# A fused LayerNorm, gated recurrence and Fourier mixing layer: the recurrence moves from a stage between two passes into the passes' tile slots

## What is computed

```python
xn    = (x - mean) / sqrt(var + eps) * ln_gamma + ln_beta        # per token
delta = sigmoid(xn @ w_delta + b_delta)                          # 16 states per token
B_t   = xn @ w_in + b_in
gate  = sigmoid(xn @ w_gate + b_gate)                            # 512 x 512
h     = tanh((h * delta[t]) @ A + B_t[t])                        # over the 2048 tokens of a sequence
x1    = layernorm(x + (h @ C) * gate + x)
w     = complex(w_freq_real, w_freq_imag)                        # 512 x 512, sparse
y     = real(ifft(fft(x1) @ w)) + bias                           # = x1 @ M + bias, with one real M
out   = layernorm(x1 + y)
```

## Time and profile before

| | |
|---|---|
| median of 3 runs (lowest, highest) | 897.38 us (897.34, 898.28) |
| profiled execution: span, which is the time it shows of itself | 897.9 us |
| PE, DVE, ACT, POOL busy | 869.1, 722.7, 566.1, 554.1 us (97%, 80%, 63%, 62%) |
| first gate product of pass A, last one's end | 23.86, 404.24 us |
| first product with M of pass B | 477.27 us |
| HBM read, written | 140.53, 67.11 MB |

### The profile page before, as it was taken

One profiled execution on the slowest core, in us unless ns is written; L12 is line 12 of the kernel. 1 busy time (PEld: TensorE's weight loads), 2 busy tenths in 40 slices (PEclk: granted clock), 3 DMA queues, 4 the chain that ended last, 5 costly groups with the idle time before them and its releaser, 6 DMA issues.

```text
span 897.9 us, 17982 instructions
## 1 busy us (share of the span) xinstructions
PE 869.1 (97%) x5275; PEld 470.4 (52%) x5306; DVE 722.7 (80%) x1510; ACT 566.1 (63%) x1063; POOL 554.1 (62%) x890
## 2 busy tenths in 40 slices
PE   7899999999999999999988999999999999999996
PEld 5354545454545444448764555555555555555553
DVE  5978888888888899885678888888888888888883
ACT  3334444444444456664645888888888888888887
POOL 2656666666665665541236677777777777777782
PEclk9999999999999999999999999999999999999999
DMA  8487788888887777526034666676677667666743
GB/s 301 141 282 281 269 295 308 323 288 287 294 297 273 272 263 263 193 95 235 1 84 147 234 227 234 241 271 217 235 259 252 218 238 272 238 233 232 259 164 141
DMA packets 94530, 210.04 MB, mean 234 GB/s; under 512 B 3616, under 2 KB 5920, under 8 KB 90528
## 3 DMA queue, kind: packets, MB, share of 16 engines
q1 hardware_dynamic: 94208, 209.41, 66.7%
q10 hardware_dynamic: 288, 0.21, 0.1%
HBM read 140.53 MB, written 67.11 MB: 231 GB/s over the span
## 4 chain that ended last, share of the span: by engine, by line
PE 54%; issue 18%; POOL 15%; DVE 7%; ACT 3%; DMA 2%; POOLq 1%; another core or an unknown queue 0%; DVEq 0%; ACTq 0%
PE bank L1344 13%; PE bank L1345 13%; PE bank L1347 13%; POOL lo_sb L711 8%; PE bank L1334 6%; PE bank L1510 3%; POOL a_rstd L698 2%; DMA x_sb<-x 2%; PE bank L1401 2%; POOL diag L706 2%; DVE bn L1002 1%; PE bank L1461 1%; PE bank L1454 1%; DVE xs_sb L1034 1%; DVE h_lo L1190 1%
## 5 line engine op out<-in xcount | busy, mean ns | idle before, releaser
L711 POOL TENSOR_TENSOR lo_sb<-xs_sb,hi_sb 128x512 f16<-128x512 f32 x128 | 150.5, 1176 | 140.0 <-ACT hi_sb L494 140.0
L754 POOL TENSOR_TENSOR x_sb<-x_sb,gate_sb 128x512 f32<-128x512 f32 x128 | 164.0, 1282 | 76.8 <-DMA x_sb<-x 60.6
L494 ACT ACTIVATE hi_sb<-xs_sb 128x512 f16<-128x512 f32 x128 | 80.6, 629 | 202.0 <-DVE xs_sb L1034 195.2
L1344 PE MATMUL bank<-wg_hi,hi_sb 128*128 128x512 f16 x512 | 194.4, 380 | 8.2 <-POOL wg_lo L716 5.6
L1345 PE MATMUL bank<-wg_lo,hi_sb 128*128 128x512 f16 x512 | 194.7, 380 | 0.0
L1344 PE MATMUL bank<-z_sb,hi_sb 128*128 128x512 f16 x512 | 194.3, 379 | 0.4 <-DVE w_ring L1241 0.4
L1345 PE MATMUL bank<-z_sb,hi_sb 128*128 128x512 f16 x512 | 194.2, 379 | 0.0
L1039 DVE SCALAR_TENSOR_TENSOR lo_sb<-bank,hi_sb 128x512 f16<-128x512 f32 x128 | 88.5, 692 | 75.5 <-ACT hi_sb L637 75.3
L1347 PE MATMUL bank<-wg_hi,lo_sb 128*128 128x512 f16 x512 | 131.4, 379 | 0.0
L1347 PE MATMUL bank<-z_sb,lo_sb 128*128 128x512 f16 x512 | 131.4, 379 | 0.0
L637 ACT ACTIVATE hi_sb<-bank 128x512 f16<-128x512 f32 x128 | 76.3, 596 | 67.8 <-PE bank L1334 67.5
(11 more groups left out here) (189 smaller groups left out, 1361.2 us busy)
## 6 DMA issues: line engine op xcount, KB each, us to landing
x_sb<-x SPq DMA_DIRECT2D x63, 1024.0 KB, 6.1
gate_dram<-gate_sb SPq DMA_DIRECT2D x32, 1024.0 KB, 5.3
gate_sb<-gate_dram SPq DMA_DIRECT2D x32, 1024.0 KB, 6.2
out<-out_sb SPq DMA_DIRECT2D x31, 1024.0 KB, 5.3
h_sb<-x_turned SPq DMA_DIRECT2D x16, 1024.0 KB, 7.3
norm_sb<-x_turned SPq DMA_DIRECT2D x15, 1024.0 KB, 7.3
h_rep<-fourier_constants SPq DMA_DIRECT2D x2, 514.0 KB, 6.1
x_sb<-x SPq DMA_DIRECT2D x2, 512.0 KB, 6.1
```

Of the source, the lines that this page charges most:

```text
L711: pool.tensor_tensor(lo_sb[:, k % 4], xs_sb[:, k % 2], hi_sb[:, k % 4], ALU.subtract).then_inc(s_lo, 1)
L754: pool.tensor_tensor(x_sb[:, k // 4, k % 4], x_sb[:, k // 4, k % 4], gate_sb[:, k // 4, k % 4], ALU.add).then_inc(s_v, 1)
L1344: nc.tensor.matmul(dst, hi_sb[:, slot_of, t], w_hi[:, t], start=(t == 0), stop=False)
```

## The change

The sequences' tokens are cut in two halves (groups) of 1024; group 0 holds partitions 0 to 63 of the state tiles and group 1 the other 64. A group's recurrence has 64 lanes by 2 column blocks, so a step still has 128 columns, and there are 32 steps for each group: 64 in all, against 32 before. The step's matrix now has a shift beside A, so that one matmul takes z and the state together (L1454 goes). One step stands in each slot: group 0 in slots 70 to 101 of pass A, group 1 in slots 5 to 36 of pass B. In a slot the matmul is the first thing on PE, tanh the first on ACT, and the product with delta the last on DVE. The check of the ends, the branch and the split into fp16 halves follow in slots 102 to 108 and 37 to 43.

M's weights are folded first (POOL, slots 52 to 66), which leaves 8 pairs of products, each of twelve matmuls of about 256 columns, in slots 85 to 111 (`PAIR_SLOTS`); ACT, DVE and POOL combine them in the slots behind. The preparations on DVE that stood in slots 104 to 124 stand in slots 48 to 80 (`PREPARATION`). Pass B's slots -7 to 2 run inside pass A's slots 121 to 130. The copies into `h_rep` are 16 DMAs for each group, in SP's order behind the gates of octet 13 and behind pass B's octet 5. The loops cover fewer octets (4 of 16 in pass A, 7 of 16 in pass B). The general rounds stay behind a branch, now one for each group.

```diff
-LANES = SEQ // CHUNK
-STEPS = 2 * CHUNK
+GROUP = SEQ // 2
+LANES = GROUP // CHUNK
...
+A_WRITTEN, B_WRITTEN, B_LAST = 5, 7, OCTETS - 2
+
+SCAN_FIRST = (70, 5)
+SCAN_CHECK = tuple(n + 2 * CHUNK for n in SCAN_FIRST)
+SCAN_BRANCH = tuple(n + 2 for n in SCAN_CHECK)
+SCAN_SPLIT = tuple(n + 1 for n in SCAN_BRANCH)
+
+PAIR_SLOTS = (85, 87, 93, 95, 101, 103, 109, 111)
...
+        m = n - TILES
+        if m >= first_b:
+            slot_b(m, m % 8, m // 8)
...
+                if v == OCTETS - 3:
+                    sp.wait_ge(s_split[0], 1)
+                    replicate_states(0)
+                    sp.dma_start(h_before[ROWS:P], h_sb[0:ROWS, :, GROUP - CHUNK:GROUP]).then_inc(s_hbefore, 16)
...
+            def scan_tanh(g, count, s):
+                act.wait_ge(s_pre[g], count)
+                nc.scalar.activation(h_sb[scan_rows(g), :, s::CHUNK],
+                                     ps_scan[g][scan_rows(g), 0:2 * LANES].rearrange("p (q l) -> p q l", q=2),
+                                     ACT.Tanh).then_inc(s_h[g], 1)
...
+            def scan_product(g, s):
+
+                rows = scan_rows(g)
+                nc.vector.tensor_tensor(zh_sb[rows, g, :, s + 1::CHUNK], h_sb[rows, :, s::CHUNK],
+                                        del_sb[rows, :, s + 1::CHUNK], ALU.mult).then_inc(s_hd[g], 1)
...
+            def scan_step(g, count, s):
+                pe.wait_ge(s_hd[g], count)
+                nc.tensor.matmul(ps_scan[g][:, 0:2 * LANES].rearrange("p (q l) -> p q l", q=2), scan_a[:],
+                                 zh_sb[:, g, :, s::CHUNK], start=True, stop=True).then_inc(s_pre[g], 1)
...
-            def slot(n, k, v):
+            def slot_b(n, k, v):
+                scan_slot(1, n)
                 if exists(n + 1):
                     transpose(n + 1, k + 1, s_bnorm, s_bhi, s_blo, s_bt)
-                if isinstance(n, int) and n + 7 < 8:
-                    first_states_out(n + 7, (k + 7) % 8)
-                elif exists(n + 7):
+                if exists(n + 7):
                     states_out(n + 7, (k + 7) % 8, v if k < 1 else v + 1)
```

More of the change, by code:

```diff
@@ L428, in second_pass @@
             def second_pass(v, q):
-                sp.wait_ge(s_v, v * 8 + 4 * q + 4)
+                if isinstance(v, int) and v == 0:
+                    sp.wait_ge(s_gst[q], 16 * OCTETS)
+                else:
+                    sp.wait_ge(s_v, v * 8 + 4 * q + 4)
                 load_gate(v + 1, q)
-                if not isinstance(v, int):
+                if before(v, 1):
                     store_result(v - 1, q)
@@ new lines, in scan_until_settled @@
+            def scan_until_settled(g):
+                act.wait_ge(s_flag[g], 1)
+                changed = act.value_load(flag[g][0:1, 0:1])
+                with act.If(changed > 0):
+                    with act.Fori(2, LANES) as r:
+                        again = act.value_load(flag[g][0:1, 0:1])
+                        with act.If(again > 0):
+                            for s in range(CHUNK):
+                                scan_tanh(g, r * CHUNK + s + 1, s)
+                            act.wait_ge(s_flag[g], r)
+                            act.sem_inc(s_round_act[g], 1)
@@ new lines, in scan_until_settled @@
+            def scan_until_settled(g):
+                changed = dve.value_load(flag[g][0:1, 0:1])
+                with dve.If(changed > 0):
+                    with dve.Fori(2, LANES) as r:
+                        again = dve.value_load(flag[g][0:1, 0:1])
+                        with dve.If(again > 0):
+                            scan_next_round(g)
+                            for s in range(CHUNK):
+                                dve.wait_ge(s_h[g], r * CHUNK + s + 1)
+                                if s + 1 < CHUNK:
+                                    scan_product(g, s)
+                            scan_compare(g, r)
+                            scan_flag(g, r)
@@ L1415, in z_transpose @@
                     pe.wait_ge(s_z, v)
[L1416 to L1419 removed]
+                if isinstance(v, int):
+                    pairs = sum(at < 8 * v + 10 for at in PAIR_SLOTS)
+                    if pairs:
+                        pe.wait_ge(s_comb, pairs)
+                for q in range(2):
+                    last = nc.tensor.transpose(ps_x[:, q * P:(q + 1) * P],
+                                               zrow[:, q].rearrange("p a b s -> p (a b s)"), ident)
@@ new lines, in scan_until_settled @@
+            def scan_until_settled(g):
+                pe.wait_ge(s_flag[g], 1)
+                changed = pe.value_load(flag[g][0:1, 0:1])
+                with pe.If(changed > 0):
+                    with pe.Fori(2, LANES) as r:
+                        again = pe.value_load(flag[g][0:1, 0:1])
+                        with pe.If(again > 0):
+                            for s in range(CHUNK):
+                                scan_step(g, r * CHUNK + s + 1, s)
+                            count_changes(g, r)
+                            pe.wait_ge(s_flag[g], r)
@@ L1482, in _ @@
-            with pe.If(changed > 0):
-                with pe.Fori(2, LANES) as r:
-                    again = pe.value_load(flag[0:1, 0:1])
-                    with pe.If(again > 0):
-                        scan_round(r * CHUNK)
-                        count_changes(r)
-                for r in range(BATCH // 2):
-                    pe.wait_ge(s_hrep2[r], 4 * 16)
-            pe.wait_ge(s_split, 1)
-            pe.wait_ge(s_c_first, 2 * BATCH)
-            def first_states_out(n, k):
-                if before(n, 2):
-                    pe.wait_ge(s_gy, n - 1)
-                halves = ((h_hi, 0), (h_hi, 1), (h_lo, 0))
-                for i, (h, c) in enumerate(halves):
-                    last = nc.tensor.matmul(ps_y[k % 2][:], h[:, 0:P], c_first[:, n, c],
-                                            start=(i == 0), stop=(i == len(halves) - 1))
-                last.then_inc(s_y, 1)
```

899 lines of the change are left out of this document (456 added, 443 removed).

## The result

The changed kernel takes 936.82 us (median of 4 runs, 933.82 to 937.29), the kernel before 897.69 beside it: a ratio of 1.0428, 95% interval 1.0408 to 1.0447. The forecast was 890 us, in a range of 872 to 901. It is slower by 39 us where a gain of 7 was expected.

A forecast was written before the change was run, and what follows sets the result against it. Both passes run at PE's pace, with a 73.0 us stage between them. Removing it from 897.9 us and adding the costs, largest 26.2 us for pass B's recurrence, gave 890.2, forecast as 890 us, range 872 to 901.

The forecast's parts named there:

- Pass B's ring: Pass B, 32 slots with steps: PE waits for DVE's product, slots grow from 3.25 to 4.07 us, adding 26.2 us.
- Recurrence in pass A: Pass A, slots 70 to 101: 32 steps at 0.25 us add 8.0 us; waits of the late ring add 6.5.
- five half octets named: Pass A's half octets without product pairs, five of eight: PE waits 1.04 us in each for DVE's late product.
- Preparations: Pass A: moved DVE work and POOL folding cost 5.0 us (bounds 2 and 9), 4.75 return; net 0.25 us.
- SP's copies in pass A: Copies ahead of the turned x of tiles 120 to 123 cost 6.7 us, clock included; bounds 0 and 9.
- the same copies have room: Pass B: SP's copies of h_rep there were priced at no cost.
- The transition: Between the passes: the 73.0 us stage goes; 2.8 us remain between last gate product and first with M.
- The last rival's rule: A matmul stream pausing every iteration can repeatedly drop to the lower clock; weighed for pass B's ring, not priced.
- The clock falls: Rival, pass B's ring: half clock for 3.4 us in every second slot, 27 us more, 917 us; chance 0.06.
- DVE sets pass A's pace: Rival, pass A: DVE's added 39 us of work costs 22 us, giving 900.5 us; chance 0.16.
- The step in pass B hides: Rival, pass B: DVE's product is ready in time, the term is 8.0 us, giving 871 us; chance 0.13.
- the signs named: Profile marks: 4.07 us transposes, five 1 us waits, late x, 2.8 us transition; over 3.1 us pass A slots disprove.

The follow-up runs named there:

- experiment 1: Changed kernel with DVE's scan product in pass B's slots moved ahead of the low half: 902.33 us, 1.0043 of the kernel before.
- Experiment 2: Changed kernel with zh_sb laid out so the 128 columns one step reads lie side by side: 924.53 us.
- experiment 7: Changed kernel with group 1's tanh written to a PSUM bank for DVE's product, a second tanh filling h_sb: 931.18 us.
- Experiment 9: Changed kernel with POOL's twelve folding adds cut to 2 columns, so M is not the reference's: 929.79 us.
- experiment 11: The five edits together, plus POOL's folding adds in other slots and C's two preparations on DVE moved to slots 114 and 115: 884.64 us.
- experiment 3: Changed kernel with SP's group 0 copies behind the turned x of tiles 120 to 123 and group 1's in three later pieces: 926.83 us.
- experiment 4: Changed kernel with group 0's copies behind the turned x and group 1's in two pieces, each behind a load of x: 924.45 us.
- the five edits together: Changed kernel with pass B's product early, step columns contiguous, pass A's ACT and DVE reordered, both groups' copies moved: 882.72 us, 0.983 of the kernel before.
- experiment 12: The five edits together, plus group 1's tanh to a PSUM bank for the product: 878.95 us, 0.980 of the kernel before.

## Why the prediction was wrong

The rings, the late turned x and most of the waits came where it put them, but it sized them too small, and it had nothing for what POOL does to DVE. The sum was 890.2 us, the profiled span 935.5. Of the 45.3 us between them 19.1 lie in pass B's ring, 7.5 in pass A's recurrence, 6.3 in slots 48 to 69, and 10.4 in two stretches of pass B that were priced at nothing.

**Pass B's ring** (forecast +27.0, measured +46.1). "The ring closes in 3.34 + 0.73 = 4.07 us" is the step that failed. Order closed it, as said (experiment 1), but 0.25 for the matmul should have been 0.50 and 0.38 for the product 0.38 and 0.89 in turn: 32 x 0.25 + 16 x 0.51 = 16.2 of the 19.1 us missed. Most of the last 3 us lies on the way from the transposes to the product, 3.46 us for 3.34. The first was there to be read. In the earlier trace rows the matmul with z (424.75), which reads every sixteenth column, has this one behind it on PE:

```profile
425.17 0.84 PE L1401 MATMUL bank<-cos_halves,out_sb 128*128 128x257 f16 x6
```

That is 0.42 us from start to start, where the matmul with the contiguous `hd` has 0.22. I took the price of a step from the latter. Experiment 2 shows 0.2 of the 0.25 to be the stride. The Trainium skill, SBUF — State Buffer, section "Door 1: The DMA port swizzle", has the rule in a note: reads that leave a 16-byte line at each element pay for it. The step's elements lay 64 bytes apart, and it paid 0.2 us. The second could not be seen in the recurrence of before, where POOL was busy 9.75 of 55.66 us and a product took 0.38; in pass B POOL was busy 72% of the time, and experiment 7 shows that beside its add the product waits.

**Recurrence in pass A** (70 to 101: forecast +21.2, measured +28.7). The miss of 7.5 us is the same 0.25 a step: 32 x 0.50 = 16.0 where I had 8.0, whose upper bound was 12.5. The waits came in the five half octets named and in none of those with a pair: PE waits there 5.4 us for `zh_sb`, for 5 x 1.04 forecast. Slots 73, 77, 81, 89 and 97 are 6.5 us over their own work, and 6.5 was the term, but that agreement is partly luck: the term has 1.2 us for slots 88 and 96, which take 3.31 us like any other with a step. The cause, too, was only partly the chain as written: POOL holding the product (1.32 us at 315.51) is a second part. The pairs cost 1.26 us each, forecast 1.34.

**Preparations** ("the net is 0.25 us"; measured 11.3 - 4.75 = 6.6). The measured 11.3 lies above the bound of 9. Experiment 9 divides it: 4.8 us go with POOL's folding, "that can hold the diagonal back", for which the term had no price of its own. The other 6.5 remain with DVE's preparations in place, and how they arise is not shown. That DVE's idle time does not take the preparations up has one sign: experiment 11 moved two of them, and their 2 us came along.

**SP's copies in pass A** (forecast 6.7, measured 8.2, within its bounds) went as predicted: the turned x was late by 5.68 us, the clock fell, and experiment 3 gave all of it back. **In pass B** "the same copies have room" was wrong by 5.8 us in the changed kernel's profile, and by 2.5 to 3.2 in those whose clock stood at 1.00 there: x and gates are loaded without spare time (experiment 4 gave back all but 0.13).

**The transition** is right: 5.88 us between the starts, of which the last gate product takes 2.8, against 2.8 + 2.8. What I did not price is that in SP's order the gates of octet 1 are loaded only when all gates are stored: slots 2 and 3 of pass B are 4.3 us too long, and DVE waits for `gate_sb` there 2.87 us (3.35 in experiment 1). Part of it goes with the clock, 0.92 in slots 0 to 4.

**The clock in pass B's ring** stayed at 1.00, as priced. The last rival's rule did not show here with PE idle 16%. None of the rivals describes the result. "The clock falls" (917) is nearest in number, and its mechanism did not occur. "DVE sets pass A's pace" (900.5) may be part of what is left in slots 48 to 69. "The step in pass B hides" is what experiment 1 made of it, with the same work in another order. Of the signs named, the five waits, the late x and the transition came; the transposes came 4.41 and 4.92 us apart and not 4.07, and slots 0 to 69 took 3.14 us on the whole and 102 to 117 3.26, both above the 3.1 that was to show the prediction wrong.

What remains open: 0.08 us of each step; why the five edits together gain 5 us less in pass A's slots 70 to 101 than was priced (the 5 in pass B's ring come back with experiment 12); what the 6.5 us in slots 48 to 69 are made of; and why the clock falls in some profiles and not in others in slots 0 to 4 and 48 to 55 of pass B.
